# Sorts with the features stationary and the one-hot rows moving, results placed by transfers, and other waits in the mixer

## The chip, the cores and the metric

The kernel runs on 1 core of one Trainium2 chip. The metric is the device time of one execution in microseconds; lower is better. Three runs of the kernel before are given, and one more execution was profiled. All clock times below are microseconds from the start of the profiled span.

## The reference

Two token blocks x (2 x 64 x 1024) go through two layers; the context is 2 x 1024 x 1024. All in float32:

```
x = x + fake_quant(layernorm(x)) @ fake_quant(ctx)             # quantised product
x = x + mamba2_mixer(layernorm(x))                             # 8 groups of 16 heads, group norm, in and out projections
x = x + base_linear(layernorm(x)) + top-2-of-8 LoRA experts    # experts
x = x + point_cloud(coords=ctx[:, :3], feats=layernorm(x))     # two attention layers over neighbours
x = x + block_masked_linear(layernorm(x))
x = x + silu-gated FFN(layernorm(x))
```

The point cloud is what the sorts serve. 1024 points of two batches (b) with 64 features each are ordered by four space-filling keys ("methods"): two Morton keys and two Hilbert keys of the quantised coordinates.

```
keys = [morton(q), morton(q_swapped), hilbert(q), hilbert(q_swapped)]
order = [argsort(k) for k in keys]                       # depends on the coordinates alone
for each of the two layers (feats, then the first layer's output):
    neigh = feats[order[window of 10 around each place]]     # for each method
    X = concat(centre, neigh - centre) over the 4 methods; heads of 64 = 16 channels x 4 methods
    attention of the 10 window rows, linear 512 -> 128, conv, instance norm, leaky relu, max over the window
```

So each layer needs its features in the four sorted orders.

## The kernel before, in words

Everything is written out by hand: five stages, each a block in which every engine has its own instruction list and waits on counting semaphores; a stage ends when all engines have ended. PSUM has eight banks of 512 float32 columns; `hold_clock` (L96 to L100) issues dummy 128x128 float32 products. Each float32 product shows as two instructions in the trace.

**Quantised product** (`stage_quantised_product`, L133). The context comes in eight chunks of 1 MB into four buffers; ScalarE scales each (L267), VectorE clips and rounds it (L230, L232, 2048 columns each), TensorE multiplies (L288). From chunk 4 on a transfer waits for a freed buffer. Behind it come the first weights w_in (L178, L180) for the ring of sixteen weight slots. At the end VectorE goes over the two halves of the result four times (L237, L242, L246 and the norm statistics L82).

**Mixer** (`stage_mixer`, L400). Eight groups g, the inner six in a hardware loop. In a group TensorE makes four projections of 128 instructions per pair (L524), turns x into PSUM banks 2 and 3 (L588), makes the output product of the *previous* group into banks 6 and 7 in two halves h (L554, `out_projection`), then Y = xs x M (L602, L606), then the segment sums of the next group (L566, needs `seg_rhs` from GpSimd, L879, `scaled_steps`). VectorE convolves (L744, L746), makes M (L815), xs = turned x times dt (L822), ranks one (method, batch) row of keys (`rank`, L762 to L781: 24 compare passes over 1024 keys, ended by the mask sum L781), adds the previous group's output to x (`after_out`, L794) and makes y_z (L833). ScalarE evacuates projections (L637, L679), applies silu and scales y to y_n (L691) once GpSimd has gated y (L896, `gated`). Rank g-1 falls into group g; the key rows are written to DRAM after the keys are done in group 0 (L912), and each row is read back by GpSimd's queue (`load_keys`, L887, with a mask chunk L888) into one buffer, behind `gated`. Between the first load and group 2, GpSimd also makes the constants of the point cloud (`cloud_constants`). The transfer of the next w_out half waits for the output product of the same half (`load_out`, L486). The last group's output product waits until x has taken the previous group's (`s_xup`), as both use banks 6 and 7.

**Experts** (`stage_lora_experts`, L926). VectorE also makes the first ten of 64 one-hot rows here.

**Point cloud** (`stage_cloud_layer`, L1277, twice). The sort: features are turned, split in two float16 parts (`spl`), and for each batch b and method m (eight in all) and each of 8 source tiles, 16 products of 64 columns (L1409) have a piece of the *one-hot* matrix (`perm`, 128x1024, made by VectorE, L1640) as weights and the features moving. The result has places on partitions; ScalarE copies it (L1552), and after each batch TensorE turns it (L1424) and ScalarE copies it into `sortedT` (L1560). The centres, repeated for the four methods, come from products with a repeat matrix (L1393) and ScalarE copies (L1546). The weights of the layer are multiplied together (L1378 to L1383) behind the first of the eight. Then GpSimd makes the first differences X (L1755), and a software pipeline of 43 steps runs: scores (L1443, L1451), turned rows (L1464), softmax on VectorE, ScalarE, GpSimd, transfers `PT<-P_turned` (L1358), weighted rows (L1480), linear (L1499, L1503), reduce.

**Point cloud output** and the **masked linear with FFN** follow and are not touched.

## Time and profile before

| | us |
|---|---|
| runs | 1100.98, 1101.09, 1105.67; median 1101.09 |
| profiled execution | 1100.37; its span 1098.7 |
| quantised product | 0 to 40.70; TensorE's last product ends at 36.0 |
| mixer | 40.70 to 493.83 |
| experts | to 517.93 |
| cloud layer 1: sort, then steps | sort 522.53 to 563.87, steps to 752.2 |
| cloud layer 2: sort, then steps | sort 756.56 to 797.39, steps to about 1014 |
| busy in one mixer group (266.30 to 314.30) | TensorE 46.93, VectorE 31.12 of 48.00 |
| keys done on VectorE | 142.0 |
| xs (L822), each of two | 0.69 |
| eight transposes of the norm at full clock (L118) | 1.11 |
| weight products of the sort | 2.08 in layer 1, 1.56 in layer 2 |
| eight centre products x 2 parts (L1393), four places | 4 x 0.87 |
| seven one-hot rows when VectorE waits for nothing (L1640) | 2.86 |
| request of a transfer on the SP queue (L1358), median | 0.59, landing 2.0 after it |

A row of a time line gives the start, the time that the merged instructions took, the engine, the line, the operation, its tiles and shapes and the count; brackets give the idle time before and what ended it. The drain is in each duration: a lone 128x64 product shows 0.19, though many in a row start 0.03 apart.

### The profile page before, as it was taken

To read this page: it belongs to the slowest core of one execution; us is meant where nothing else is said; L and a number is where in the kernel's file an instruction comes from. 1 tells how busy PE (TensorE), PEld (TensorE's weight loads), DVE (VectorE), ACT (ScalarE), POOL (GpSimd) and SP (SyncE) were. 2 spreads that over 40 slices of the span, in tenths; PEclk is the share of its full clock that TensorE was granted. 3 is DMA by queue.
4 is the path that set the end of the run, shared out by engine and by line. 5 is a ranking of instruction groups with operands and counts; after the bars stand their busy time and mean duration, and the time that the engine had idled before them with its cause. 6 is when DMAs were issued, how large, how long until landed. Compare 5 with 4: busy or idle time off the path is not lost. (4 is left out here: it accounts for less than half of the span.)

```text
span 1098.7 us, 38438 instructions
## 1 busy us (share of the span) xinstructions
PE 1009.8 (92%) x16165; PEld 766.2 (70%) x16165; DVE 781.2 (71%) x1982; ACT 436.0 (40%) x639; POOL 440.0 (40%) x414
## 2 busy tenths in 40 slices
PE   4699998999999999669998999998989999998898
PEld 1499868696877869335986777768876666665585
DVE  7699887566466767835758999976668888896410
ACT  5222212130422213202346777762347777773010
POOL 1101163020211202200048999970069888886000
PEclk9899999999999999979999999999999999999999
DMA  8996686876868782544102222221012222221560
GB/s 326 395 373 251 250 294 232 297 288 248 327 246 315 261 306 74 184 200 187 50 8 64 70 69 67 67 73 27 4 26 67 58 57 57 59 60 37 194 266 19
DMA packets 56313, 177.18 MB, mean 161 GB/s; under 512 B 9017, under 2 KB 9769, under 8 KB 55850
## 3 DMA queue, kind: packets, MB, share of 16 engines
q1 hardware_dynamic: 53802, 167.60, 43.8%
q0 software_dynamic: 2432, 8.42, 2.1%
q8 instruction: 62, 1.02, 0.4%
q14 instruction: 17, 0.14, 0.0%
HBM read 150.26 MB, written 0.56 MB: 137 GB/s over the span
## 5 line engine op out<-in xcount | busy, mean ns | idle before, releaser
L524 PEld LDWEIGHTS ps<-hT,ring 128*128 128x128 f32 x2304 | 259.1, 192 | 9.5 <-ACT xpad L637 5.8
L524 PE MATMUL ps<-hT,ring 128*128 128x128 f32 x2304 | 260.3, 275 | 4.9 <-ACT xpad L637 4.9
L1774 POOL TENSOR_TENSOR X<-sortedT,ring 128x960 f16 (+1 forms) x84 | 155.9, 1856 | 0.0
L896 POOL TENSOR_TENSOR y_y<-y_z,sgate 128x512 f32<-128x512 f32 x16 | 20.0, 1270 | 218.2 <-DVE y_z L833 218.2
L1792 POOL TENSOR_TENSOR S<-S,den 128x480 f32<-128x480 f32 x86 | 85.7, 996 | 36.0 <-DVE den L1712 36.0
L554 PE MATMUL ps<-wt,y_n 128*128 128x512 f32 x224 | 99.1, 595 | 0.0
L1480 PE MATMUL ps<-PT,ring 128*64 128x120 f16 x2752 | 96.4, 221 | 2.6 <-DMA PT<-P_turned 2.3
L1799 POOL TENSOR_TENSOR PP<-S,PP 128x480 f16<-128x480 f32 x86 | 96.8, 1126 | 3.5 <-ACT PP L1582 3.5
L1480 PEld LDWEIGHTS ps<-PT,ring 128*64 128x64 f16 x2752 | 81.8, 110 | 15.6 <-DMA PT<-P_turned 5.8
L1582 ACT CAST PP<-S 128x480 f16<-128x480 f32 x86 | 66.8, 777 | 61.2 <-POOL S L1792 54.9
L1568 ACT COPY OT<-ps 128x960 f32<-128x960 f32 x86 | 81.2, 944 | 16.4 <-PE ps L1480 16.4
L1574 ACT COPY ring<-ps 128x1024 f16<-128x1024 f16 x86 | 87.3, 1015 | 0.0
L1499 PE MATMUL ps<-OT,WN 128*128 128x480 f32 x172 | 76.3, 566 | 0.0
L554 PEld LDWEIGHTS ps<-wt,y_n 128*128 128x128 f32 x224 | 41.5, 190 | 46.9 <-issue 46.9
L1688 DVE TENSOR_REDUCE mx<-ps 128x16 f32<-128x480 f32 x86 | 55.7, 648 | 22.8 <-PE ps L1451 20.1
L1670 DVE BATCH_NORM_STATS2 stats<-ps 128x240 f32 (+2 forms) x129 | 47.9, 399 | 30.7 <-PE ps L1499 21.3
L1589 ACT ACTIVATE S<-S 128x480 f32<-128x480 f32 x86 | 51.4, 598 | 44.7 <-DVE S L1690 44.7
L1703 DVE STREAM_TRANSPOSE P_turned<-PP 128x512 f32<-128x512 f32 x86 | 60.7, 706 | 9.0 <-PE ps L1480 6.7
L691 ACT ACTIVATE y_n<-y_y,parg 128x128 f32<-128x128 f32 x56 | 17.5, 390 | 122.0 <-POOL y_y L896 122.0
L746 DVE SCALAR_TENSOR_TENSOR xc<-xpad,parg,xc 128x128 f32<-128x128 f32 x192 | 64.7, 398 | 1.7
L1409 PEld LDWEIGHTS ps<-ring 128*128 128x128 f16 x2048 | 61.4, 98 | 1.6
L1710 DVE TENSOR_REDUCE den<-S 128x16 f32<-128x480 f32 x86 | 55.9, 650 | 8.6 <-ACT S L1589 5.1
(319 smaller groups left out, 1663.7 us busy)
## 6 DMA issues: line engine op xcount, KB each, us to landing
ring<-in_w_in SPq DMA_DIRECT2D x36, 2048.0 KB, 8.0
wt<-in_w_out SPq DMA_DIRECT2D x16, 2048.0 KB, 7.9
PT<-P_turned SPq DMA_DIRECT2D x344, 64.0 KB, 2.0
ctx_chunks<-in_ctx SPq DMA_DIRECT2D x8, 1024.0 KB, 7.2
ring<-in_w SPq DMA_DIRECT2D x8, 1024.0 KB, 12.4
krow<-keys_scratch POOLq DMA_DIRECT2D x8, 512.0 KB, 7.7
mchunk<-in_mask_t POOLq DMA_DIRECT2D x8, 512.0 KB, 8.7
ring<-in_base_w SPq DMA_DIRECT2D x1, 4096.0 KB, 17.4
```

The lines of the kernel that those rows point to most:

```text
L524: mm = nc.tensor.matmul(ps[:, bank, j * T:(j + 1) * T], weights[:, j, kc * P:(kc + 1) * P], k.hT[:, kc, :], start=kc == 0, stop=kc == KC - 1)
L554: mm = nc.tensor.matmul(ps[:, 6 + c, :], rows[:, j, :], k.wt[:, j, c * HALF:(c + 1) * HALF], start=j == 0, stop=j == GB - 1)
L746: ins = vec.scalar_tensor_tensor(out=dst, in0=src, scalar=params(j, tap), in1=dst, op0=ALU.mult, op1=ALU.add)
L1409: mm = nc.tensor.matmul(ps[:, (i + halves[0]) % 2, pt * C:(pt + 1) * C], c.perm[:, perm_buffer(layer, j), pt * P:(pt + 1) * P], c.spl[:, s ...
L1480: mm = nc.tensor.matmul(ps[half, O_BANK + slot // 4, at:at + 4 * ROWS], XR[:, slot, half], PT[:, :, r * SLOTS + slot, 0:ROWS, part], start ...
L1499: mm = nc.tensor.matmul(H, c.WN[:, a, 0, :], OT[:, a, :, :], start=False, stop=a == 1)
L1568: sc.copy(c.OT[ph % 2][:, :, :, :].rearrange("p a b n -> p a (b n)"), ps[:, O_BANK:O_BANK + 2, 0:2 * COLS]).then_inc(s_O, 1)
L1574: sc.copy(c.XR[ph][:, :, :].rearrange("p s d -> p (s d)"), xt[ph % 2]).then_inc(s_XR, 1)
L1582: sc.copy(c.PP[ph % 2][:, :, 0:ROWS, 0], c.S[ph % 2][:, :, :]).then_inc(s_hi, 1)
L1774: ins = gp.tensor_tensor(fcopy(c.X[u][:, 0, 0:1], full(cnt)), fcopy(c.fsT[:, 0, bass.ds(it * STEP, 1)], trio(start, cnt, 1)), fcopy(c.fTr[ ...
L1792: gp.tensor_tensor(S, S, fcopy(c.den[ph % 2][:, :], [[1, 2 * SLOTS], [0, ROWS]]), ALU.mult).then_inc(s_P, 1)
L1799: gp.tensor_tensor(PP[:, :, 0:ROWS, 1], c.S[ph % 2][:, :, :], PP[:, :, 0:ROWS, 0], ALU.subtract).then_inc(s_lo, 1)
```

## The change

1. *Sorts.* The eight (batch, method) rounds become four rounds of one method with both batches. The features are the weights (128x64, batch b on output partitions 64b to 64b+63) and the one-hot rows move, 512 columns at a time. The order of the one-hot rows alternates the batches. The result has channels on partitions: ScalarE copies it in two halves into one of two buffers (`sorted`), and transfers of 16 partitions each place it in `sortedT`: eight of 4 KB rows per method, and for the last method eight heads (four on the SP, four on ScalarE's queue, between ScalarE's two copies) and eight tails. Transposes, repeat matrix and centre products go; the rows are stored to DRAM once and read back repeated into `fTr`. The first differences are one instruction. The layer's weight products go first, ahead of the transposes.
2. *Mixer.* rank(g-1) goes ahead of xs, after_out(g-1) behind y_z, its reciprocal right behind y_z. The last group's output product goes to banks 0 and 1 and waits no more for x. GpSimd makes the segment input of group 2 ahead of the key transfers and the constants.
3. *Quantised product.* Eight chunk buffers (four of them in the ring) instead of four; the end of the stage is two passes instead of three, with the bias added to x beforehand; 40 clock-holding products at its end.

```diff
 def stage_quantised_product(nc, k, dr):
-    CHUNKS, BUFS, KPC = 8, 4, 2
+    CHUNKS, BUFS, KPC = 8, 8, 2
+        early = k.sb("ctx_chunks", [P, BUFS // 2, KPC, D], F32, ctx)
+        cbuf = [early[:, i] for i in range(BUFS // 2)] + [k.ring[:, 8 + KPC * i:8 + KPC * (i + 1), :] for i in range(BUFS // 2)]
...
             for j in range(4):
+                if j >= 2:
+                    sp.wait_ge(s_q2, CHUNKS // 2 + 2 * (j - 1))
...
+            nc.vector.tensor_tensor(off[:, 0:1], off[:, 0:1], s12[:, :], ALU.mult).then_inc(s_q1, 1)
+            v.wait_ge(s_q1, 7)
+            nc.vector.tensor_tensor(rowb[:, 0:1], rowb[:, 1:2], s12[:, :], ALU.mult).then_inc(s_q1, 1)
+            v.wait_ge(s_q1, 8)
+            nc.vector.tensor_scalar(k.x[:, :], k.x[:, :], rowb[:, 0:1], None, ALU.add).then_inc(s_q1, 1)
...
+            hold_clock(nc, k, 0, 8 * HOLD)
...
-            def out_projection(g, h, rows, before_h1=variance):
-                if h == 0:
+            def out_projection(g, h, rows, before_h1=variance, bank=6):
+                if h == 0 and bank == 6:
                     pe.wait_ge(s_xup, 2 * g)
...
             for h in range(2):
-                out_projection(NG - 1, h, xc)
-            hold_clock(nc, k, 0, 2 * HOLD)
+                out_projection(NG - 1, h, xc, bank=0)
+            hold_clock(nc, k, 2, 2 * HOLD)
...
-                if final:
+                if not first:
                     rank(g - 1)
                 for h in range(2):
                     v.wait_ge(s_xT, 2 * g + h + 1)
...
-                if not first and not final:
-                    rank(g - 1)
-                    after_out(g - 1)
                 v.wait_ge(s_Y, g + 1)
...
+                if not first:
+                    inverse(g - 1)
+                if not first and not final:
+                    after_out(g - 1)
...
             gated(0, True)
+            scaled_steps(2, False)
             pool.wait_ge(s_key, KEY_STEPS)
...
             cloud_constants(nc, pool, k, k.cloud)
-            with pool.Fori(1, NG - 1) as g:
+            gated(1, False)
+            load_keys(1, False)
+            with pool.Fori(2, NG - 1) as g:
...
     j = j if layer == 1 else PRODUCTS - 1 - j
-    return j // (NM * NT), j // NT % NM, j % NT
+    return j % B, j // (B * NT), j // B % NT
...
+        def place_sorted(eng, i, b, a, r, cols):
+            at, to = b * C + (a * 2 + r) * CH, r * C + methods[i] * CH
+            return eng.dma_start(c.fsT[to:to + CH, a * B + b, cols], c.sorted[i % 2][at:at + CH, cols])
...
+            for a in range(2):
+                for b in range(B):
+                    at, to = b * C + a * 2 * CH, (a * B + b) * 2 * CH
+                    sp.dma_start(c.rows_kept[to:to + 2 * CH, :], src[at:at + 2 * CH, :]).then_inc(c.kept, 16)
+            sp.wait_ge(c.kept, 64 * layer)
+            for r in range(2):
+                for m in range(NM):
+                    to = r * C + m * CH
+                    sp.dma_start(c.fTr[to:to + CH, :, :],
+                                 bass.AP(tensor=c.rows_kept.tensor, offset=c.rows_kept.offset + r * CH * N,
+                                         ap=[[N, CH], [2 * CH * N, 2 * B], [1, N]])).then_inc(s_cc, 16)
...
+            for i in range(NM - 1):
+                sp.wait_ge(s_row, row0 + 2 * (i + 1))
+                for b, a, r in heads:
+                    place_sorted(sp, i, b, a, r, slice(0, N)).then_inc(s_sc[i], 16)
+            sp.wait_ge(s_row, row0 + 2 * NM - 1)
+            for b, a, r in heads[:4]:
+                place_sorted(sp, NM - 1, b, a, r, slice(0, HALF)).then_inc(s_head, 16)
+            sp.wait_ge(s_row, row0 + 2 * NM)
+            for b, a, r in heads:
+                place_sorted(sp, NM - 1, b, a, r, slice(HALF, N)).then_inc(s_tail, 16)
...
-                    for pt in range(NT):
+                    for half in range(2):
                         for s in range(2):
-                            mm = nc.tensor.matmul(ps[:, (i + halves[0]) % 2, pt * C:(pt + 1) * C], c.perm[:, perm_buffer(layer, j), pt * P:(pt + 1) * P],
-                                                  c.spl[:, s, t, b * C:(b + 1) * C], start=at + pt + s == 0,
-                                                  stop=at == NT - 1 and pt == NT - 1 and s == 1)
+                            for x in range(B):
+                                b = sort_order(layer, j + x)[0]
+                                mm = nc.tensor.matmul(ps[b * C:(b + 1) * C, bank + half, :], c.spl[:, s, t, b * C:(b + 1) * C],
+                                                      c.perm[:, perm_buffer(layer, j + x), half * HALF:(half + 1) * HALF],
+                                                      start=at + s == 0, stop=at == NT - 1 and s == 1)
                     mm.then_inc(s_ord, 1)
...
+                act.wait_ge(s_ord, ord0 + NT * (i + 1))
+                if i >= 2:
+                    act.wait_ge(s_sc[i - 2], head0 + 16 * 8)
                 for half in range(2):
+                    sc.mul(c.sorted[i % 2][:, half * HALF:(half + 1) * HALF], ps[:, bank + half, :], 1 / SCALE).then_inc(s_row, 1)
+                    if i == NM - 1 and half == 0:
+                        act.wait_ge(s_row, row0 + 2 * NM - 1)
+                        for b, a, r in heads[4:]:
+                            place_sorted(act, i, b, a, r, slice(0, HALF)).then_inc(s_head, 16)
```

## Rows read from the trace of the kernel before

**Rows 1.** The page, engine table: busy time, share of the span, instructions.
```profile
PE 1009.8 (92%) x16165; PEld 766.2 (70%) x16165; DVE 781.2 (71%) x1982; ACT 436.0 (40%) x639; POOL 440.0 (40%) x414
```
**Rows 2.** Time line of TensorE, mixer's group 7 and last output product.
```profile
451.87 0.25 PE L602 MATMUL ps<-ones_col,xs 128*64 128x1 f32 x2 [2.54 <-issue]
...
474.89 8.87 PE L554 MATMUL ps<-wt,xc 128*128 128x512 f32 x16 [14.62 <-DVE x_sb L794]
```
**Rows 3.** Time line of VectorE, the mixer's last rank pass and end.
```profile
458.70 1.28 DVE L774 TENSOR_SCALAR_CACHE_REDUCE junk<-krow,kcol 128x1024 bf16<-128x1024 f32 x1 [2.93 <-DMA krow<-keys_scratch]
...
472.11 1.21 DVE L781 TENSOR_REDUCE msum<-mchunk 128x32 f32<-128x1024 int32 x1
...
492.27 1.28 DVE L82 BATCH_NORM_STATS2 bn<-x_sb 128x6 f32<-128x512 f32 x2
```
**Rows 4.** Time line of TensorE, projections of groups 6 and 7.
```profile
377.79 14.56 PE L524 MATMUL ps<-hT,ring 128*128 128x128 f32 x128 [0.93 <-ACT xpad L637]
...
410.23 14.45 PE L524 MATMUL ps<-hT,ring 128*128 128x128 f32 x128
```
**Rows 5.** VectorE's y_z of group 6; then the landing times of w_out (L486).
```profile
416.93 2.15 DVE L833 SCALAR_TENSOR_TENSOR y_z<-xsil,parg,ps 128x128 f32<-128x128 f32 x8
...
DMA to landing us min/median/max: 7.6/7.9/13.3
```
**Rows 6.** Time lines in group 1; the landing line is that of krow (L887).
```profile
148.93 0.60 POOL L887 DMA_DIRECT2D krow<-keys_scratch  x1 [4.15 <-DMA keys_scratch<-w_rows]
...
DMA to landing us min/median/max: 4.3/7.7/8.6
...
157.53 1.28 DVE L774 TENSOR_SCALAR_CACHE_REDUCE junk<-krow,kcol 128x1024 bf16<-128x1024 f32 x1
...
171.76 1.22 DVE L781 TENSOR_REDUCE msum<-mchunk 128x1024 int32 x1
...
168.18 3.48 PE L566 MATMUL ps<-seg_rhs,tri_gt 128*128 128x512 f32 x4 [3.99 <-POOL seg_rhs L879]
171.50 4.74 PE L524 MATMUL ps<-hT,ring 128*128 128x128 f32 x41
```
**Rows 7.** Time lines, end of the quantised product and the mixer's first transposes.
```profile
32.82 1.23 DVE L232 TENSOR_SCALAR q<-ctx_chunks 128x2048 bf16<-128x2048 f32 x1
...
36.63 1.28 DVE L242 TENSOR_TENSOR wt<-ps,wt 128x512 f32<-128x512 f32 x2
...
42.45 1.97 PE L118 MATMUL ps<-ident,h_sb 128*128 128x128 f32 x8 [6.44 <-DVE h_sb L93]
```
**Rows 8.** Groups by line, 522 to 563 (count, busy us, mean ns, idle before).
```profile
L1409 PE MATMUL ps<-ring 128*128 128x64 f16 x1024 | 30.8, 193 | 0.0
...
L1393 PE MATMUL ps<-P_turned,repeats 128*128 128x512 f16 x16 | 4.1, 379 | 0.0
```
**Rows 9.** Time line of TensorE, products of 64 weights' columns in pairs.
```profile
591.96 1.12 PE L1480 MATMUL ps<-PT,ring 128*64 128x120 f16 x32
...
1017.60 3.60 PE L1832 MATMUL ps<-ring,conv_last 128*64 128x512 f32 x8 [2.68 <-PEq L1280]
```
**Rows 10.** Busy by stretch; last columns granted clock, transfer share, GB/s.
```profile
520.00:524.00 4.00, 4.00 (x75) 3.99 (x74) 2.09 (x4) 3.06 (x5) 0.00 (x0) 1.00 1.02 367
...
760.00:761.00 1.00, 1.00 (x22) 1.00 (x19) 1.00 (x4) 0.50 (x1) 0.00 (x0) 1.00 0.80 187
...
590.00:598.00 8.00, 7.45 (x234) 5.53 (x234) 7.18 (x15) 6.24 (x9) 8.00 (x7) 1.00 0.36 86
```
**Rows 11.** Time line of TensorE, first and third scores, layers 1 and 2.
```profile
563.87 0.28 PE L1443 MATMUL ps<-mask_cols,mask_rows 64*128 64x240 bf16 x2 [0.19 <-POOL X L1755]
...
571.58 0.28 PE L1443 MATMUL ps<-mask_cols,mask_rows 64*128 64x240 bf16 x2
...
797.39 0.28 PE L1443 MATMUL ps<-mask_cols,mask_rows 64*128 64x240 bf16 x2 [0.19 <-POOL X L1755]
...
804.27 0.28 PE L1443 MATMUL ps<-mask_cols,mask_rows 64*128 64x240 bf16 x2 [0.73 <-POOL X L1774]
```

More of the change, by code:

```diff
@@ L233, in _ @@
             v.wait_ge(s_mm, 1)
-            v.wait_ge(s_q1, 6)
+            v.wait_ge(s_q1, 9)
             for h in range(2):
                 cols = slice(h * HALF, (h + 1) * HALF)
-                nc.vector.tensor_scalar(tsum[:, cols], csum(h), off[:, 0:1], rowb[:, 1:2], ALU.mult, ALU.add).then_inc(s_fin, 1)
+                nc.vector.scalar_tensor_tensor(out=tsum[:, cols], in0=csum(h), scalar=off[:, 0:1], in1=k.x[:, cols],
+                                               op0=ALU.mult, op1=ALU.add).then_inc(s_fin, 1)
             v.wait_ge(s_mm, 2)
@@ L241, in _ @@
                 v.wait_ge(s_fin, h + 1)
[L242 to L246 removed]
+                nc.vector.scalar_tensor_tensor(out=k.x[:, cols], in0=acc(h), scalar=s12[:, 0:1], in1=tsum[:, cols],
                                                op0=ALU.mult, op1=ALU.add).then_inc(s_fin, 1)
             for h in range(2):
[L249 removed]
+                v.wait_ge(s_fin, h + 3)
                 norm_statistics(nc, k, Norm(k, 1), h)
@@ L1248, in __init__ @@
         self.fsg = slots(7, 2).rearrange("p (t d) -> p t d", t=NT)
+        self.sorted = [k.ring[:, 7 + u, :] for u in range(2)]
         self.W = N + WIN - 1 - LEAD
@@ L1312, in stage_cloud_layer @@
         xt = [ps[:, bank, :].bitcast(F16) for bank in XT_BANK]
-        parts = [c.PC[u][:, :, :, :].rearrange("p s i w -> p (s i w)") for u in range(2)]
         block = ctx.enter_context(nc.Block())
@@ L1363, in _ @@
         def _(pe):
-            hold_clock(nc, k, 7, HOLD)
-            if layer == 1:
-                norm_tensor(nc, pe, k, n)
-            else:
-                for i in halves:
-                    for j in range(4):
-                        mm = nc.tensor.transpose(ps[:, i, j * P:(j + 1) * P], src[:, (4 * i + j) * P:(4 * i + j + 1) * P], k.ident[:, :])
-                    mm.then_inc(s_turn, 1)
+            hold_clock(nc, k, 5, HOLD)
             def weight_products():
@@ L1383, in weight_products @@
                     nc.tensor.matmul(ps[:, 7, 0:KC * 32], c.blocks[:, :], k.msum[:, :], start=True, stop=True).then_inc(s_sum, 1)
-            def centres(ab):
-                pe.wait_ge(s_wc, wc0 + 3)
-                for half in range(2):
-                    g = 2 * ab + half
-                    if g >= 2:
-                        pe.wait_ge(s_cc, cc0 + g - 1)
-                    for s in range(2):
-                        mm = nc.tensor.matmul(ps[:, 4 + half, :], c.sel[:, ab, :], parts[s][:, half * HALF:(half + 1) * HALF], start=s == 0, stop=s == 1)
-                    mm.then_inc(s_ct, 1)
-            hold_clock(nc, k, 7, 2 * HOLD)
-            for i, (b, m) in enumerate(order):
+            weight_products()
+            if layer == 1:
+                norm_tensor(nc, pe, k, n)
+            else:
+                for i in halves:
+                    for j in range(4):
+                        mm = nc.tensor.transpose(ps[:, i, j * P:(j + 1) * P], src[:, (4 * i + j) * P:(4 * i + j + 1) * P], k.ident[:, :])
+                    mm.then_inc(s_turn, 1)
+            hold_clock(nc, k, 5, 2 * HOLD)
+            for i in range(NM):
+                bank = 2 * ((i + 1) % 2)
                 if i >= 2:
-                    pe.wait_ge(s_row, row0 + i - 1)
+                    pe.wait_ge(s_row, row0 + 2 * (i - 1))
                 for at in range(NT):
-                    j = i * NT + at
+                    j = (i * NT + at) * B
                     t = sort_order(layer, j)[2]
@@ L1649, in edges @@
             def edges():
-                v.wait_ge(s_sc, sc0 + 8)
+                for i in range(NM - 1):
+                    v.wait_ge(s_sc[i], head0 + 16 * 8)
+                v.wait_ge(s_head, head0 + 16 * 8)
+                v.wait_ge(s_tail, tail0 + 16 * 8)
                 row = c.W
@@ L1804, in step @@
                 low_part(*lagged(0))
-            first_differences()
+            differences(0, 0)
             differences(1, 1)
```

125 lines of the change are left out of this document (43 added, 82 removed).

## The prediction

> **What bounds the kernel now.** I read the engine table first, then the time lines of TensorE, VectorE, GpSimd and the transfer queue over each stage that the diff touches. The table [rows 1] has TensorE busy for 1009.8 of 1098.7 us, so there is little idle time to win except in a few places; the time lines show where they are. The chain of waits reaches back only through the last stage, which the change leaves alone, so it decides nothing here.
>
> The largest hole is at the mixer's end. TensorE starts the output product of group 7 at 474.89 after 14.62 us of idle time, and its first half takes 8.87 us for 7.1 [rows 2]. VectorE shows why: the last rank pass starts at 458.70 and its mask sum ends at 473.32; only behind them does it add group 6's result to x, and the product of group 7 goes to the same two banks [rows 3]. Inside the mixer a group takes TensorE 48.0 us, of which 0.93 to 1.14 us are a wait for ScalarE's copy xpad [rows 4]; ScalarE is late because VectorE ranks (some 14.5 us) ahead of y_z. In the sorts TensorE has no hole: 1024 products of 64 columns at about 29 ns take 30.8 us of layer 1's [rows 8].
>
> **Profiled time and runs.** Span 1098.7, execution 1100.37, median of the runs 1101.09. I sum against the execution and add 0.7 for the median.
>
> **1. Quantised product, to the start of the mixer's group 2.** All eight chunks are requested at once, so w_in no longer shares the queue with the last ones. But VectorE needs 2 x 1.23 us per chunk; with three new small operations ahead (0.15 + 0.15 + 0.8, with their waits about 1.15) it starts at 13.1 and ends the last chunk at 32.9 in place of 34.05. Behind it, six passes over 512 columns less two of 0.64 each [rows 7]: VectorE would be done at 37.8. TensorE, which ended its last product at 36.0 and now does at 34.8, then runs 40 clock-holding products; at 0.11 us each (128 of that shape take 14.45, [rows 4]) they end at 39.3, and the stage ends with them: 1.2 us earlier. The clock stays up, so the eight transposes take 1.1 (as at the other stages' starts) in place of 1.97 [rows 7] and VectorE's part of group 0, which has no idle time of note up to the keys at 142, starts 2.2 earlier. The weights arrive in the order of use and are no bound: the queue is never empty in either version.
>
> In group 1 this gain is lost. rank(0) now stands ahead of xs. Its key row is requested at 148.93 - 2.2 = 146.7 and, with 4.3 to 8.6 us to landing, is there at about 154; the pass with its mask sum took from 157.53 to 172.98, 15.45 [rows 6]. So xs (two of 0.69) ends at 154 + 15.45 + 1.3 = 170.8, where it stood ahead of the pass before. TensorE reached this point at 162.8 (168.18 less the wait of 3.99 and 1.3 of small products), now at 160.6: it waits 10 us. Before, it waited 3.99 us a step later for seg_rhs, which GpSimd made only behind its constants; that wait goes, since the step is moved ahead of them (it waits for segments(1), 117.4, and delays nothing: the keys come at 140). At half clock the small products (1.3) and the segment product (1.98) come to 5.0, as the old 3.48 shows: group 2's projections start at 175.8, not 171.50: **+4.3** (bounds +2.5 with an early key row, +6).
>
> **2. Groups 2 to 6.** VectorE ranks after M and is free for xs 8 us before TensorE asks; y_z then comes right behind Y; before, it started at 416.93, 6.7 us into the next group's projections [rows 4, 5], ScalarE's chain moves forward and the xpad wait ends: 4 x 0.93 = **-3.7**. Nothing takes its place: TensorE has 47.1 us of work a group, VectorE some 31, the key row is loaded over 20 us ahead of its use. Bounds -3.7 and 0.
>
> **3. Group 7 and the tail.** Count from the start of its projections (410.23; the stage ends at 493.55, 83.3 later). New: projections 28.8, turned halves with their wait 1.9, variance and first half of product 6: 37.9. xs no longer keeps TensorE waiting (2.54 before, [rows 2]); Y ends at 39.2, second half of product 6 at 46.3, first half of product 7 at 53.4, since it has banks of its own. Its last weights are requested at 46.3 and need 7.6 to 13.3 us [rows 5]; the two last took about 8.9: 55.2. Second half: 62.3. The last rank pass runs from 43.4 (mask sum of rank(6) at 35.3, request and landing 8.1) to 57.9, under it. Then 1.41 and 1.28 for x and its statistics as before [rows 3]: 65.0. **-18.3** (bounds -19 and -14, by the landing). The experts' weights are requested behind s_out 14 as before and land at 67.6, when they are wanted at 68.4.
>
> **4. The sorts.** Weight products (14 and 2 instructions, 2.08 us in layer 1, 1.56 in layer 2) go ahead of the transposes, so the sort begins 1.9 and 1.6 later. It loses eight centre products (3.46), four groups of transposes and their copies. The product itself: 256 of 512 columns per layer in pairs on the two column halves. Do pairs run together? [rows 9]: 32 products of 64x120 take 1.12 us, less a drain of 0.22 this is 29 ns each, where 120 columns alone at full clock need 50. The last layer's 8 instructions of 64x512 f32 take 3.60 us at half clock while one takes 1.05: starts 0.85 us apart in pairs. So 128 pairs at 0.217 (what the 16 single 512-column products took, [rows 8]) = 27.8 us. VectorE makes the one-hot rows at 0.40 each when not waiting, 0.8 per pair against 0.87: not a bound.
>
> The Trainium skill (TensorE: Matmul & The Clock Gate, Part 3, The mechanism) says that a weight load overlaps running products only where its row group differs; here all use all rows, and by its 53 ns per 64-column load the sorts would grow by 2 x 13.7 us. The trace speaks against it: loads of 98 ns stand under products 28.5 ns apart.
>
> Now the transfers. Each method's rows go out in 8 transfers of 64 KB to 16 partitions each, and ahead of them in the same queue 8 of 256 KB make the repeated centres, also 16 partitions each. What rate? [rows 10]: writing 128 partitions the engines moved 367 GB/s at a busy share of 1.02 (360 at full share), writing 64 partitions 187 at 0.80 (234), writing 32 partitions 86 at 0.36 (239). For 16 no row exists: above 235, below half of that, 118, the rate per partition of the 32 case, which I take as the nearest. Then in layer 1 the centres (2.1 MB, requested from 528.3, behind the zeros and the round trip through DRAM) move until 547.3, set 0 until 551.7, set 1 until 556.2. The copy of method 2 reuses buffer 0: it waits until 552.4 instead of 545.3, that of method 3 until 556.9 instead of 552.4 (the sort starts at 524.4 and takes 27.8). Set 2 is issued at 0.59 each from 553.6 to 558.3, the heads after it to 560.7, landed 563.5. differences(0) takes 1.87: scores from 565.5 against 563.87 before [rows 11]: +1.6. Layer 2, without the zeros: centres 757.8 to 775.6, copies of f16 777.8, sets 0 and 1 782.2 and 786.6, heads landed 794, scores from 796.0 against 797.39 [rows 11]: -1.4. TensorE idles for over 7 us ahead of the scores, so they start at half clock; before, layer 1 lost 0.8 that way already (7.71 us from the first to the third scores against 6.88, [rows 11]). I put 1.5 and 2.3 on it (the estimate: the first step's and a group of clock-holding products at half clock; less in layer 1, which had part of it). Sum: **+4.0**.
>
> The Trainium skill (SBUF — State Buffer, Door 1: The DMA port swizzle) gives about 109 GB/s for partitions 0 to 15 and the same rate for 32 as for 64 partitions; the trace agrees on the latter. By 109 both layers come 2 us later: 1091.
>
> The tails of method 3 are issued from 558 on and land before differences(2), 5.1 us behind the first; costs nothing.
>
> **Sum:** 1100.4 + 4.3 - 3.7 - 18.3 + 4.0 = 1086.7, with 0.7: **1087**.
>
> **Rivals.**
> - *The placements keep up* (235 GB/s). Centres end at 538.5, no copy waits, heads land at 557.2, scores 4.7 and 4.4 us earlier, less 1.5 and 2.3 for the clock: -5.3, total 1078. For it: 32 and 64 partitions have one rate. Against: 128 has another. 25%.
> - *The port figure* of the sentence above, 1091. 10%.
> - *Slower: the halves don't run together.* 256 x 0.217 = 55.6 us per sort, the transfers then hidden: 1078 + 2 x 27.8 = 1133. It decides if a pair costs over 0.33 us. Against it both rows of [rows 9]. 4%. With bare weight loads (2 x 13.7 on 1078) 1105, 3%.
> - *The mixer gives back more:* key row 2 us later and the last weights at 13.3: +7, 1094. 8%.
>
> The forecast itself (1081 to 1093) has 50%. Range for 8 in 10: **1075 to 1099**. A difference below 0.5%, 5.5 us, is about what can't be told from none. Faster by more: forecast, placements, port figure: 0.84; same 0.09; slower 0.07.
>
> **What would show it.** TensorE's idle time between the last two output products under 3 us; a wait of about 10 us ahead of L602's counterpart in group 1 and none for xpad later; 40 more L100 products. In the sorts: 64-column products with starts 0.217 us apart per pair; ScalarE's third and fourth copies waiting for a transfer (rival: for TensorE); the share of the transfer engines near 1 at about 120 GB/s over 17 us. A third copy that waits for nothing refutes the step on rates; a period over 0.33 us the pairing; a group over 47.5 us the step on the mixer.

## The result, and the profile after

The changed kernel takes 1090.75 us (median of 4 runs, 1089.31 to 1091.21) beside 1103.34 for the kernel before in the same comparison; the ratio is 0.9876, 95% interval [0.9851, 0.9902]. The forecast of 1087.0 against 1101.09 is a ratio of 0.9872. The profiled execution took 1089.31 with a span of 1087.7, which is 11.0 less than the span before; the forecast for it was 13.7 less. Stage by stage (from the first instruction of TensorE in each stage; scores are those of the layer's first step):

| | before | after | difference | forecast |
|---|---|---|---|---|
| start to projections of group 2 | 171.50 | 184.85 | +13.35 | +4.3 |
| groups 2 to 6 | 238.73 | 233.99 | -4.74 | -3.7 |
| group 7 to the end of the mixer | 83.65 | 65.07 | -18.58 | -18.3 |
| experts | 24.09 | 24.09 | 0 | 0 |
| layer 1: start to scores | 45.90 | 47.40 | +1.50 | +1.6 |
| layer 1: scores to end | 188.40 | 189.84 | +1.44 | +1.5 |
| layer 2: start to scores | 45.12 | 41.75 | -3.37 | -1.4 |
| layer 2: scores to end | 220.21 | 218.89 | -1.32 | +2.3 |
| last two stages | 81.10 | 81.82 | +0.72 | 0 |

The total was met by luck: two errors of opposite sign cancel. The start of the mixer cost 9 us more than forecast, the sorts and steps 5.8 less.

The engine table after, as [rows 1]:

```profile
PE 1001.1 (92%) x14613; PEld 738.6 (68%) x14613; DVE 780.2 (72%) x1981; ACT 418.5 (38%) x605; POOL 439.4 (40%) x406
```

The time line of TensorE after:

```profile
34.39 9.09 PE L100 MATMUL ps<-ident 128*128 128x128 f32 x80
...
119.33 28.75 PE L530 MATMUL ps<-hT,ring 128*128 128x128 f32 x256
...
163.94 1.11 PE L594 MATMUL ps<-ident,xsil 128*128 128x128 f32 x4 [5.03 <-ACT xsil L649]
...
180.32 0.34 PE L608 MATMUL ps<-ones_col,xs 128*64 128x1 f32 x2 [5.70 <-DVE xs L832]
...
184.85 28.75 PE L530 MATMUL ps<-hT,ring 128*128 128x128 f32 x256
...
418.84 28.75 PE L530 MATMUL ps<-hT,ring 128*128 128x128 f32 x256
...
466.69 7.11 PE L560 MATMUL ps<-wt,xc 128*128 128x512 f32 x16 [1.79 <-DMA wt<-in_w_out]
...
473.77 7.11 PE L560 MATMUL ps<-wt,xc 128*128 128x512 f32 x16
```

These rows show three things. The 14.62 us hole of [rows 2] has become a wait of 1.79 us for weights. The group whose projections ran in two parts with 0.93 us between them [rows 4] now runs 256 instructions in one row. And group 2 starts 13.35 us later than at 171.50 [rows 6], behind the waits shown and 80 holding instructions.

VectorE in group 1 before:

```profile
147.04 1.11 DVE L744 TENSOR_SCALAR xc<-xpad,parg 128x128 f32<-128x128 f32 x4
```

VectorE after, in the quantised product and in group 1:

```profile
36.37 1.28 DVE L82 BATCH_NORM_STATS2 bn<-x_sb 128x6 f32<-128x512 f32 x2
...
150.58 7.85 DVE L751 TENSOR_SCALAR xc<-xpad,parg 128x128 f32<-128x128 f32 x4
158.47 4.75 DVE L753 SCALAR_TENSOR_TENSOR xc<-xpad,parg,xc 128x128 f32<-128x128 f32 x12
163.14 1.21 DVE L825 TENSOR_TENSOR MT<-decay,gm 128x1024 f32<-128x1024 f32 x1
...
178.80 1.28 DVE L832 TENSOR_TENSOR xs<-ps,dt_tok 128x512 f32<-128x512 f32 x2
```

GpSimd after, in group 1:

```profile
149.75 0.60 POOL L900 DMA_DIRECT2D krow<-keys_scratch  x1 [1.40 <-DMA keys_scratch<-w_rows]
...
150.87 1.86 POOL L1219 MEMSET X<- 128x1024 f16 x2
...
156.76 1.01 POOL L1222 IOTA iota<- 128x1024 f16 x1
```

VectorE is done with the quantised product at 37.65, while TensorE holds the clock until 43.48. In group 1 four convolution instructions took 7.85 us, where the same four took 1.11 us before. The first of the four alone took 7.28 us, from 150.58 to 157.86: it was held as long as GpSimd's row of fills ran, from 150.87 to the end of the iota at 157.77.

The sort of layer 1, TensorE, then ScalarE's third and fourth copies:

```profile
514.39 27.23 PE L1445 MATMUL ps<-ring 128*64 128x512 f16 x250
542.04 0.84 PE L1445 MATMUL ps<-ring 128*64 128x512 f16 x6 [0.43 <-issue]
555.40 0.39 PE L1466 MATMUL ps<-mask_cols,mask_rows 64*128 64x240 bf16 x2 [12.52 <-POOL X L1781]
```

```profile
542.95 1.08 ACT L1568 ACTIVATE ring<-ps 128x512 f32<-128x512 f32 x2 [13.43 <-PE ps L1445]
545.19 0.60 ACT L1568 ACTIVATE ring<-ps 128x512 f32<-128x512 f32 x1 [1.16 <-DMA sortedT<-ring]
```

256 products of 512 columns take 28.5 us, 0.22 per pair, as read from [rows 9]. The third copy's own products were done near 535.8 (three quarters of the way from 514.39), so what it waited for until 542.95 was the buffer of the first method, though the row names TensorE; in the same place of hold15 and no_hold (below) the row names `DMA sortedT<-ring`.

The transfer summaries of three stretches after (centres of layer 1, centres of layer 2, placements of layer 2 behind them):

```profile
DMA packets 586, 1.89 MB, mean 118 GB/s; under 512 B 124, under 2 KB 124, under 8 KB 586
```

```profile
DMA packets 612, 1.80 MB, mean 129 GB/s; under 512 B 125, under 2 KB 125, under 8 KB 612
```

```profile
DMA packets 586, 1.17 MB, mean 212 GB/s; under 512 B 250, under 2 KB 250, under 8 KB 586
```

Centres moved at 118 and 129 GB/s, for the 118 forecast for 16 partitions. Placements, also to 16 partitions each, moved at 212 in layer 2, which is why its scores come earlier than forecast. In layer 1 they were slower, above the forecast all the same (539 to 543):

```profile
DMA packets 317, 0.65 MB, mean 163 GB/s; under 512 B 158, under 2 KB 158, under 8 KB 317
```

### The profile page after: what moved, and what is told of

The parts are those of the page before. It is cut to its first block and busy times, and to the rows that moved or that the text cites. A ratio compares the mean times of both kernels' runs of the same rounds, so it can differ in the third digit from the quotient of the medians.

```text
span 1087.7 us, 35385 instructions
## 1 busy us (share of the span) xinstructions
PE 1001.1 (92%) x14613; PEld 738.6 (68%) x14613; DVE 780.2 (72%) x1981; ACT 418.5 (38%) x605; POOL 439.4 (40%) x406
## 5 line engine op out<-in xcount | busy, mean ns | idle before, releaser
L1781 POOL TENSOR_TENSOR X<-sortedT,ring 128x960 f16 (+2 forms) x86 | 159.9, 1860 | 124.3 <-DMA sortedT<-ring 124.3
L560 PE MATMUL ps<-wt,y_n 128*128 128x512 f32 x224 | 101.5, 607 | 0.0
L100 PE MATMUL ps<-ident 128*128 128x128 f32 x460 | 59.4, 288 | 5.1 <-PEq L1293 2.8
L100 PEld LDWEIGHTS ps<-ident 128*128 128x128 f32 x460 | 57.0, 203 | 9.7 <-issue 8.6
L751 DVE TENSOR_SCALAR xc<-xpad,parg 128x128 f32<-128x128 f32 x64 | 33.1, 688 | 36.2 <-ACT xpad L643 35.2
## 6 DMA issues: line engine op xcount, KB each, us to landing
ring<-in_w SPq DMA_DIRECT2D x8, 1024.0 KB, 12.8
```

The source lines that it names most:

```text
L100: nc.tensor.matmul(k.ps[:, bank, 0:P], k.ident[:, :], k.ident[:, :], start=True, stop=True)
L560: mm = nc.tensor.matmul(ps[:, bank + c, :], rows[:, j, :], k.wt[:, j, c * HALF:(c + 1) * HALF], start=j == 0, stop=j == GB - 1)
L1781: ins = gp.tensor_tensor(fcopy(c.X[u][:, 0, 0:1], full(cnt)), fcopy(c.fsT[:, 0, bass.ds(it * STEP, 1)], trio(start, cnt, 1)), fcopy(c.fTr[ ...
```

## The experiments

Each is a kernel with the edit shown, on the kernel named (the changed one where none is), beside runs of the kernel before on the same chip. Ratios are to the kernel before, with 95% intervals; the changed kernel has 0.9876. "Group 2" is the start of its projections.

**No holding products** (`no_hold`).

```diff
-            hold_clock(nc, k, 0, 8 * HOLD)
```

> The changed kernel without the 40 clock-holding products at the end of the quantised product. Theory: they are 80 instructions at 0.114 us and run until 43.48, while VectorE is done with the stage at 37.65, so they alone hold the stage open. Without them it ends at about 38.6; the eight transposes cost 1.97 again in place of 1.10; everything up to group 1 comes about 4.0 earlier (group 1's projections start at 115.3 in place of 119.33), and the profiled execution is near 1085.3 in place of 1089.31. Rival: group 1 gives it back, since its wait for xs hangs on something that does not move along (the key row's landing); then the projections of group 1 start earlier but those of group 2 still at about 184.8, and the execution stays near 1089.

Measured: 1084.14 us, ratio 0.9806 [0.9758, 0.9855], span 1083.0. Group 2 starts at 178.83 instead of 184.85. TensorE, GpSimd and VectorE:

```profile
173.07 0.34 PE L607 MATMUL ps<-ones_col,xs 128*64 128x1 f32 x2 [10.38 <-DVE xs L831]
```

```profile
149.20 0.60 POOL L899 DMA_DIRECT2D krow<-keys_scratch  x1 [4.58 <-DMA keys_scratch<-w_rows]
```

```profile
146.85 1.11 DVE L750 TENSOR_SCALAR xc<-xpad,parg 128x128 f32<-128x128 f32 x4
...
152.53 4.73 DVE L770 COPY kcol<-keys 128x8 f32 x1
```

The convolution takes 1.11 us again: GpSimd waited 4.58 us for the key rows to reach DRAM instead of 1.40, so its fills begin at 150.32, behind the convolution, and not at 150.87 in the middle of one that started 3.7 us later. The fills still meet VectorE, on the small copy `kcol` ahead of the rank pass: 4.73 us for 0.28. Most of that lies under the landing of the key row (requested at 149.20, 6.5 us to landing), so it delays the rank pass, which starts at 157.29, by only 1 to 1.6 us. Then the wait for xs is 10.38 us, for a forecast of 10. The gain of 6.0 at group 2 is made of 2.0 at the start of group 1 (4.9 in group 0, less products at half clock in between) and 4.0 in group 1. The theory's time came out (profiled 1084.65 for 1085.3), but it had put all of the gain ahead of group 1.

**Constants ahead of the keys** (`early_constants`).

```diff
+            cloud_constants(nc, pool, k, k.cloud)
             pool.wait_ge(s_key, KEY_STEPS)
...
-            cloud_constants(nc, pool, k, k.cloud)
```

> The changed kernel with GpSimd's constants of the point cloud ahead of its wait for the keys (they run from about 128 to 145 instead of 151 to 167). Theory: VectorE's second tap-0 convolution of group 1 (four instructions, 7.85 us in the changed kernel against 1.11 before) was slow because GpSimd's fills ran at the same time; it falls back to about 1.1, xs of group 1 comes about 6.7 earlier (rank(0) then waits 0 to 2 us for its key row), and group 2's projections start at about 178 to 180 in place of 184.85: execution about 1083 to 1084.5. First rival: the slow convolution has another cause (transfers, the instruction stream): it keeps about 7.8 us and the execution 1089. Second rival: VectorE's key steps, which now run beside the fills, get slower by as much: the keys end 3 us or more later and under 3 us are gained.

Measured: 1090.8, 0.9883 [0.9809, 0.9958], single runs 1086.86 to 1099.97, group 2 at 187.36. VectorE:

```profile
127.64 7.69 DVE L360 TENSOR_SCALAR w_m<-w_q 128x32 int32<-128x32 int32 x1
...
154.66 0.25 DVE L396 STREAM_TRANSPOSE w_rows<-keys 128x64 f32<-128x64 f32 x1
...
159.97 1.11 DVE L751 TENSOR_SCALAR xc<-xpad,parg 128x128 f32<-128x128 f32 x4
```

The convolution is back at 1.11, and the key steps, which now run beside the fills, end at 154.9 instead of 145.5; 1.2 us of that were there ahead of the fills. The second rival holds: the fills cost VectorE some 8 us in both places, here nearly all of it in one tensor-scalar of 128x32 that takes 7.69 us where its like takes 0.18. The Trainium skill (SBUF — State Buffer, Who interferes with whom) has the rule: VectorE and GpSimd share a pair of ports under an exclusive lock, and where a copy or tensor-scalar in a two-port mode meets a GpSimd instruction, whichever was issued second is blocked for the whole of the other. The traces agree on the blocking: the convolution takes 7.85, 7.88 and 8.11 us in the three kernels in which fills run beside it, 1.11 in those where they don't. They show more than one instruction's length, though: a single VectorE instruction stayed blocked through a whole row of back-to-back GpSimd instructions, in the changed kernel (freed at 157.86, with the iota ended at 157.77), in this one (135.33, with the last memset of the row ended at 135.29) and, on the `kcol` copy, in no_hold (157.26, with the iota ended at 157.22).

**The sorts alone** (`sorts_alone`): the changed kernel with `stage_quantised_product` and `stage_mixer` of the kernel before.

```diff
-    CHUNKS, BUFS, KPC = 8, 8, 2
+    CHUNKS, BUFS, KPC = 8, 4, 2
...
-            hold_clock(nc, k, 0, 8 * HOLD)
...
-                if not first:
+                if final:
                     rank(g - 1)
```

> The changed kernel with the quantised product and the mixer of the kernel before: only the sorts differ from the kernel before. Theory: the stage differences of the two traces carry over: scores of layer 1 start 1.5 later from the stage's start (47.4 for 45.9), steps of layer 1 +1.4, layer 2's scores 3.4 earlier (41.75 for 45.12 from its start), steps of layer 2 -1.3, end +0.7: in sum -1.0, execution near 1099.4, no difference that can be measured. Rival: the sorts as such gain more, or lose, and the difference of the traces comes from where the stages start in the clock's pattern: then the sum lies outside -3 to +1.

Measured: 1098.66, 0.994 [0.9917, 0.9962], span 1095.8, that is 2.9 less than before: layer 1's scores +0.3 (46.19 from the stage's start), its steps +0.4, layer 2's scores -3.9, its steps -0.15, the end +0.7. The spans put the gain at the edge of what was allowed to the theory (-3 to +1). The medians put it beyond: 1098.66 beside 1104.85 in the same comparison, as the profiled execution of the kernel before is one of its faster ones. So the sorts gain 3 to 6 us, and the forecast's +4.0 for this part is refuted.

**The tail alone** (`tail_alone`): the kernel before with the last output product in banks 0 and 1.

```diff
-                out_projection(NG - 1, h, xc)
+                out_projection(NG - 1, h, xc, bank=0)
...
-                if h == 0:
+                if h == 0 and bank == 6:
                     pe.wait_ge(s_xup, 2 * g)
```

(with the reciprocal of group 6 behind y_z and ScalarE's wait for it, as in the changed kernel)

> The kernel before with one edit: the last group's output product goes to banks 0 and 1 and does not wait for x. Theory: TensorE goes on at about 460.3 instead of 474.89 and has both halves done at about 476.5, with the last rank pass (458.70 to 473.32) under them; x and its statistics follow until about 479.3, so the mixer ends 14.3 earlier: execution near 1086.1. The remaining 4 us of the 18.6 that the changed kernel gains in group 7 then belong to the order of rank, xs and y_z in the groups. Rival: all 18.6 belong to this edit (execution 1081.8), or the last weights land late and it gives under 11.

Measured: 1089.58, 0.986 [0.9812, 0.9908], span 1087.7. From group 7's projections (412.30) to the end of the mixer (483.12) it takes 70.8 us, 12.8 less than before:

```profile
463.67 7.03 PE L554 MATMUL ps<-wt,xc 128*128 128x512 f32 x16
...
472.96 7.13 PE L554 MATMUL ps<-wt,xc 128*128 128x512 f32 x16 [2.15 <-DMA wt<-in_w_out]
```

14.3 were expected; the last weights (a wait of 2.15 us) and some products at half clock (1.98 for 1.16 in Y) took the rest. The groups keep their old period here, 47.85 us on average from group 2 to 7 (173.03 to 412.30). This edit by itself gives as much as the whole change does.

**Centres cut wide** (`centres_wide`).

```diff
-            for r in range(2):
-                for m in range(NM):
-                    to = r * C + m * CH
-                    sp.dma_start(c.fTr[to:to + CH, :, :],
...
-                                         ap=[[N, CH], [2 * CH * N, 2 * B], [1, N]])).then_inc(s_cc, 16)
+            for q in range(2 * B):
+                for r in range(2):
+                    sp.dma_start(c.fTr[r * C:(r + 1) * C, q, :],
...
+                                         ap=[[0, NM], [N, CH], [1, N]])).then_inc(s_cc, 16)
```

> The changed kernel with the eight transfers of the repeated centres cut another way: 64 partitions x one 4 KB row each instead of 16 partitions x four rows; the same 2 MB, packets and order in the queue. Theory: the rate follows the number of partitions written (120 to 129 GB/s for 16, about 235 for 64): centres take about 9 us instead of 17, no copy of the sort waits for a placement, and the scores start about 4 us earlier in layer 1 (43 to 44 us after the stage's start, for 47.4) and about 2 in layer 2 (its last copy waited for TensorE already); execution about 1083 to 1085 for 1089.31. Rival: the rate is limited at the DRAM side or by the size of the rows, whatever the partitions: centres stay at 120 to 130 GB/s and nothing moves.

Measured: 1098.45, 0.996 [0.9941, 0.9978]. Slower than the changed kernel; both theory and rival missed. The stretch's last columns are the granted clock, the share of the 16 transfer engines and GB/s, as in [rows 10]; then SP's issues:

```profile
528.00:530.00 2.00, 2.00 (x22) 0.96 (x18) 2.00 (x7) 0.00 (x1) 0.00 (x0) 1.00 0.25 98
```

```profile
520.94 8.59 SPq L1369 DMA_DIRECT2D ring<-cloud_rows  x8
```

A share of 0.25 is four engines of 16: 98 GB/s over four is 24.5 each, where the sixteen of the changed kernel moved 7.5 each. The outermost dimension of the new source is the fourfold repeat, and that many engines were used. The Trainium skill (DMA: Bandwidth & Descriptors, Rules for kernel authors) warns of just this, that a leading zero-stride broadcast of c copies confines a transfer to c engines; the trace agrees. So the run doesn't test the theory on partitions. It shows only that each of the four engines moved three times what each of sixteen did; why is left open.

**Rank behind xs, in group 1 alone** (`group1_late`, on no_hold).

```diff
-                if not first:
+                if not first and not late:
                     rank(g - 1)
...
+                if late:
+                    rank(g - 1)
...
-            with v.Fori(1, NG - 1) as g:
+            group(1, False, late=True)
+            with v.Fori(2, NG - 1) as g:
```

> The changed kernel without the 40 holding products (as no_hold, 1083.0 span) and, in group 1 alone, rank(0) behind xs instead of ahead of it; groups 2 to 7 as changed. Theory: the wait of TensorE for xs in group 1 (10.38 us in no_hold) is made by this order alone; it goes, and group 2's projections start at about 168 to 170 in place of 178.83; of that up to 2 us come back in group 2, where y_z is late and ScalarE's xpad with it. Span about 1074 to 1076. Rival: without that wait something else holds group 1 (the segment input, the key row) and group 2 still starts after 175; span above 1080.

Measured: 1069.79, 0.9697 [0.9672, 0.9723], span 1068.7, 14.3 less than no_hold. Group 2 starts at 164.76, before even the lower end of what was expected, and the groups behind it keep 46.8 us:

```profile
161.38 0.28 PE L607 MATMUL ps<-ones_col,xs 128*64 128x1 f32 x2
...
164.76 17.47 PE L529 MATMUL ps<-hT,ring 128*128 128x128 f32 x155
```

No wait stands ahead of the first row. Besides the 10.38 us, Y and the segment products run at full clock again (1.16 for 1.98).

**Rank behind xs in groups 1 to 6** (`rank_after_xs`, on the changed kernel).

```diff
-                if not first:
+                if final:
                     rank(g - 1)
...
+                if not first and not final:
+                    rank(g - 1)
```

> The changed kernel with rank(g-1) behind xs in groups 1 to 6, as in the kernel before; x still takes the output product behind y_z. Theory: the period of groups 2 to 6 goes from 46.83 back to about 47.8, for y_z is late and TensorE waits 0.9 for xpad again (+4.7 over five groups); in group 1 TensorE no longer waits for xs (-8 to -13 with the slow convolution's share): group 2 starts near 174; together 4 to 8 less than the changed kernel: 1082 to 1086. Rival: x behind y_z already frees ScalarE's chain and the period stays at 46.9: then execution 1077 to 1080, and the order of rank and xs is worth nothing in groups 2 to 6.

Measured: 1083.54, 0.9809 [0.975, 0.9868] (single runs 1077.34 to 1093.28). Group 2 starts at 178.84 and group 7 at 412.83: 46.80 per group. The rival holds on the period; its execution of 1077 to 1080 came in two of the four runs. The xpad wait is ended by x being updated behind y_z, not by rank's new place: y_z follows rank directly, without the 1.41 us of x between them, and begins 4.8 us into the next group's projections here and 6.5 before. VectorE here, then before:

```profile
230.48 2.15 DVE L842 SCALAR_TENSOR_TENSOR y_z<-xsil,parg,ps 128x128 f32<-128x128 f32 x8
```

```profile
224.83 2.15 DVE L833 SCALAR_TENSOR_TENSOR y_z<-xsil,parg,ps 128x128 f32<-128x128 f32 x8
```

(the groups began at 225.67 and 218.33). So rank's move ahead of xs gained nothing in groups 2 to 6 and cost 6 us or more in group 1.

**Fifteen holding products** (`hold15`, and with group1_late's order `hold15_late`).

```diff
-            hold_clock(nc, k, 0, 8 * HOLD)
+            hold_clock(nc, k, 0, 15)
```

> The changed kernel with 15 clock-holding products instead of 40 at the end of the quantised product: they end at about 37.8, with VectorE. Theory: the stage ends near 38.6 as without any, and the clock stays up, so the eight transposes take 1.1 (1.97 without) and the stage's first projections 3.5; group 1's projections start 4.8 earlier than in the changed kernel (114.5 for 119.33). Rival: by group 1 the clock's pattern has levelled this, as it did without any hold (4.9 earlier in group 0, 2.0 in group 1): 117. The execution is 1081 by the first, 1084 by the second, if group 1 goes as in no_hold; with the convolution of group 1 slow again, 1086 to 1089.

> group1_late with 15 clock-holding products at the end of the quantised product (hold15's edit and group1_late's together). Theory: the edits touch different waits; hold15 was 5.5 us of span below no_hold, of which 1.4 lay ahead of group 2 and the rest in the sorts' and steps' clock: span near 1063 to 1067 against 1068.7 of group1_late. Rival: the rest was chance of where the stages start in the clock's pattern, and the two are equal within 2: 1067 to 1070.

Measured: 1079.12, 0.9781 [0.9756, 0.9805], group 1 at 116.47, group 2 at 177.44; and 1067.75, 0.967 [0.9649, 0.969], span 1066.3. For hold15 the rival on group 1 holds (117 forecast). Against no_hold group 2 comes 1.4 earlier. The ratios lie 0.0025 (hold15 against no_hold) and 0.0027 (with the late rank, against group1_late) lower, some 3 us, but both pairs of intervals overlap: a hold cut to end with VectorE is harmless, and a gain from it is not shown.

**Centres in another order, on two queues, and in small pieces** (`centres_alternate`, `centres_two_queues`, `centres_small`, each on group1_late).

```diff
-            for r in range(2):
-                for m in range(NM):
+            for m in range(NM):
+                for r in range(2):
```

On two queues, the transfers of r = 0 are issued by SP and those of r = 1 by ScalarE. In small pieces, the queues are the same and each makes 16 transfers, one row per partition in each (`fTr[to:to + CH, q, :]`).

> group1_late (span 1068.7) with the eight centre transfers in another order: methods outside, channel halves inside, so that neighbours in the queue write partitions 0-15 and 64-79 in turn instead of 0-15, 16-31; shape, bytes and count as in the changed kernel. Theory: what limits them to 120 to 129 GB/s is that all 16 transfer engines write into the same group of partitions at a time, and the placements get 190 to 240 because theirs alternate between two far groups: the centres then move at 190 or more, are done in 11 us for 17, and the scores of layer 1 start about 3 earlier from the stage's start (42 for 45.1). Rival: the engines keep step, so that each transfer still has one group of partitions to itself, or the limit is at the DRAM side: 120 to 130 GB/s as before, nothing moves.

> group1_late with the four centre transfers of channel half 1 (partitions 64 to 127) issued on ScalarE's queue, beside the other four on SP's. Theory: two queues are served in turn, so two groups of partitions are written at once: 190 to 240 GB/s over the centres, and layer 1's scores 3 to 4 earlier from the stage's start (41 to 42 for 45.1), less what four issues (4 x 0.5 us) on ScalarE delay its first copy, which has over 1 us of room. Rival: the limit is the source (rows read back from DRAM): 120 to 130 GB/s with two queues as well.

> As centres_two_queues (half 0 on SP's queue, half 1 on ScalarE's), but each transfer cut to what a placement is, 16 partitions x one 4 KB row: 2 x 16 transfers for 2 x 4; destination and shape are then those of the placements, and only the source differs (rows in DRAM). Issuing allows some 290 GB/s. Theory: the placements' 190 to 240 GB/s came from small pieces that alternate between far partitions, so the centres now reach 190 or more while they are alone in the queues, and the scores of layer 1 come 1 to 3 earlier from the stage's start than there (41.97), if ScalarE's longer issuing (7.5 us ahead of its first copy) doesn't eat it. Rival: what limits them is reading rows back from DRAM: 120 to 130 GB/s again, and scores at 42 to 44.

| | us, ratio | centres, GB/s | scores of layer 1 from the stage's start |
|---|---|---|---|
| group1_late | 1069.79, 0.9697 | 115 to 131 | 45.12 |
| alternate | 1068.13, 0.9675 [0.9651, 0.9699] | 117 to 129 | 45.60 |
| two queues | 1063.30, 0.9631 [0.9612, 0.9651] | 115 to 135 | 41.97 |
| small pieces | 1065.08, 0.9654 [0.9623, 0.9684] | 166 to 180 | 42.08 |

The stretch 506 to 508 of two queues and of small pieces:

```profile
506.00:508.00 2.00, 2.00 (x22) 1.02 (x20) 1.96 (x6) 0.00 (x0) 0.00 (x0) 1.00 1.03 125
```

```profile
506.00:508.00 2.00, 2.00 (x22) 1.03 (x20) 2.00 (x6) 0.00 (x0) 0.00 (x0) 1.00 1.07 168
```

The order changes nothing. Two queues don't raise the rate of the centres either, yet bring the scores 3.2 us forward: the third copy, which waits for the first placements, comes 23.4 us behind the sort's start instead of 26.2, and from 510 to 520 the stretches show 162 to 215 GB/s. That placements run there beside what is left of the centres is the likely reading; the summaries don't part the two. Small pieces do raise it, from the same rows in DRAM, so the source doesn't set 120. But with two queues transfers to two groups of partitions are outstanding together, and small pieces on one queue were not run, so whether the 16 partitions set it stays open. Their scores come no earlier, since the fourth copy now waits for its products:

```profile
523.86 0.60 ACT L1574 ACTIVATE ring<-ps 128x512 f32<-128x512 f32 x1 [5.16 <-PE ps L1445]
```

From the last product (523.83) to the scores 7.8 us are left, which no faster centre can take away. Both of these kernels beat the changed one (0.9876) and the one before.

## Why the prediction was right, and where it was not

**Step 3, the tail: right.** 65.07 us for 65.0. The product has banks of its own and the rank pass lies under it. The wait for weights is 1.79 us, as long as forecast, but stands ahead of the first half and not between the halves. By tail_alone 12.8 of the 18.6 belong to the banks. Of the other 5.8, 3.6 are waits that tail_alone still has in group 7 (1.12 for xpad, 2.52 ahead of the xs product), 1.5 its products at half clock and 0.4 its weights.

**Step 2: right in size, wrong in cause.** The wait for xpad went in every group that had it, 4.74 us over groups 2 to 6 for 3.7 forecast (0.2 us a group of other small waits went too). The prediction put it on VectorE ranking ahead of xs. rank_after_xs shows the period of 46.80 with rank where it was, and tail_alone 47.85 with x where it was: x's update behind y_z does it.

**Step 1: wrong, +13.35 for +4.3.** Two terms failed. Of the 9.05 us, 4.25 were there at the start of group 1 (117.28 before, 119.33 after, for 2.2 earlier in the forecast) and 4.8 arose in it.
- *"40 clock-holding products; at 0.11 us each (128 of that shape take 14.45, [rows 4]) they end at 39.3"*. Each float32 product is two instructions, and [rows 4] counts instructions: 80 of them took 9.09 us. The stage ended 2.8 us later instead of 1.2 earlier. This is a slip in reading a count that the front of this document states itself.
- *That the key row's landing decides when rank(0) starts.* The forecast put that at about 154. It started at 164.59, behind a convolution that met GpSimd's fills (7.85 us for 1.11) and that has no term in the forecast. The fills begin when GpSimd's wait for the keys to reach DRAM ends. That wait was 4.15 us in [rows 6], 1.40, 1.46 and 1.91 in the three kernels with the 40 holds and the constants in their place, and 2.60 to 4.58 in the seven with a shorter hold or none. All three of the former had the collision on the convolution, none of the latter. So it came with the holds; why the wait is shorter with them stays open.

What was forecast of the order itself, "it waits 10 us", is what no_hold shows: 10.38, of which the fills on `kcol` make 1 to 1.6. In the changed kernel the wait was shared out: 5.03 for xsil, 5.70 for xs. And with rank behind xs group 2 starts 14 us earlier.

**Step 4, the sorts: pairs, centres and layer 1 right; layer 2's placements and its clock term wrong.** Layer 1: the sort began 1.8 later (forecast 1.9), the third copy came 28.6 us behind the sort's start (28.0), the scores 41.0 (41.1). In layer 2 the third copy came at 23.6 (24.0, the landing of set 0), but the fourth had nothing to wait for but its products, as set 1 was placed at 212 GB/s and not at 118; scores 35.85 behind the sort's start for 37.8. The rival of placements at 235 was nearer for layer 2's placements (212) and wrong for the centres; layer 1's placements (163) lie between the two. Forecast and rival had costed centres and placements at one rate. One sum of the forecast doesn't close: 2.1 MB at 118 GB/s from 528.3 end at 546.1 and not at 547.3; against the 41.1 us to the scores that is small.

The two terms for the half clock were 1.5 and 2.3. From first to third scores layer 1 took 8.13 us for 7.71 and layer 2 8.27 for 6.88 [rows 11]. All kernels run here have the same code from the scores on, so their traces can be compared. In layer 1 that stretch takes 188.40 and 188.68 us in the two with the old sort, 188.78 to 192.23 in the twelve with the new one (mean 190.3): the term of 1.5 is of the right size. In layer 2 it takes 220.21 and 219.24 with the old sort, 217.73 to 221.17 with the new (mean 219.3): the term of 2.3 is not borne out. There the late start is absorbed: by the sixth step the lead over the kernel before was back at 10.35 of the initial 10.40.

**The rivals.** The halves do run together (a pair 0.22 us); weight loads did not stand bare (256 products with their loads in 28.5 us). The centres at 118 and 129 GB/s speak against the rival of 109. "The mixer gives back more" was the one that came about: 7 us were its price and 7.7 the measured excess of the whole mixer, through other mechanisms than those named.

## What to carry to other kernels

When work moves ahead of a step that another engine waits for, cost the first round by itself: its inputs are often the latest of all, and a loop that gains 1 us in each later round can lose 10 in the first. Here the gain did not even need the move. Count a timing filler in instructions of the trace: 40 holding products that outlast the other engine cost 6 us at group 2 here, and what fifteen give back was too little to show. Before moving a chunk of GpSimd fills or VectorE copies, look at what the other engine runs in that window.

## What the runs showed of the hardware

- A row of GpSimd fills blocked one VectorE instruction until the row's end: a 128x128 float32 tensor-scalar for 7.28 us (four of them 7.85 for 1.11), a 128x32 integer one for 7.69 (0.18 otherwise), a 128x8 copy for 4.73 (0.28 otherwise).
- Transfers to 16 partitions moved at 118 to 129 GB/s with four rows of 4 KB for each partition, and at 166 to 180 with one row each on two queues, from the same rows in DRAM; placements of one row each between SBUF partitions moved at 163 in layer 1 and 212 in layer 2.
- A transfer whose outermost dimension was a repeat of four kept four of the sixteen engines busy, at 98 GB/s.
